# A graph layer's loads, products and exponentials put in another order: staged x ahead of the stores, the first products in hn, a first burst ahead of the second late halves

## What is computed

```python
h = relu(bn(conv1d(xT, conv1_w, pad=0)))               # 1 tap
h = bn(conv1d(h, conv2_w, pad=8))                      # 17 taps
x_conv = relu(h + xT).T
s = x @ w_se.T + b_se                                  # 3 features
dist = sq_i + sq_j - 2 * s @ s.T
A = exp(-dist) * mask
msg = relu(x @ w_msg.T + b_msg)
x_in = concat([x_conv, A @ msg])
gi = x_in @ w_ih.T + b_ih
gh = x @ w_hh.T + b_hh
r, z = sigmoid(gi_r + gh_r), sigmoid(gi_z + gh_z)
n = tanh(gi_n + r * gh_n)
out = layernorm(x + (1 - z) * n + z * x)
```

## Time and profile before

| | |
|---|---|
| median of 3 runs | 332.51 us (330.48 to 332.54) |
| profiled execution | 333.4 us |
| its span, first to last instruction | 331.3 us |
| TensorE busy | 300.3 us (91%) |
| VectorE busy | 248.8 us (75%) |
| ScalarE busy | 154.3 us (47%) |
| mean granted clock of TensorE | 0.977 |
| moved by DMA | 27.21 MB, 82 GB/s over the span |

### The profile page before, as it was taken

How to read it: one execution, slowest core, us unless ns; L and a number is a source line. 1 busy time by engine, 2 the same in 40 slices (tenths; PEclk the granted TensorE clock), 3 DMA queues, 4 the chain that set the end, 5 groups by cost and what they waited for, 6 DMA issues and landing times.

```text
span 331.3 us, 4634 instructions
## 1 busy us (share of the span) xinstructions
PE 300.3 (91%) x1408; PEld 240.1 (72%) x1408; DVE 248.8 (75%) x667; ACT 154.3 (47%) x321; POOL 26.0 (8%) x53
## 2 busy tenths in 40 slices
PE   2859889969999999998999999999999999999970
PEld 1647758748888777886888777887888678888850
DVE  3384869944895996973995996974996996964686
ACT  4564724325776422425876422426776513324440
POOL 3300000000000013000000013000000022000122
PEclk9989999996999999999999999999999999999996
DMA  6600152360121032064120022082110041150002
GB/s 171 249 0 3 28 193 96 85 210 29 59 65 32 32 96 97 33 201 158 57 62 32 32 89 101 32 267 107 61 41 30 32 127 63 38 152 0 0 32 95
DMA packets 12687, 27.21 MB, mean 82 GB/s; under 512 B 1538, under 2 KB 2180, under 8 KB 12548
## 3 DMA queue, kind: packets, MB, share of 16 engines
q1 hardware_dynamic: 12676, 27.08, 24.6%
HBM read 22.88 MB, written 4.19 MB: 82 GB/s over the span
## 4 chain that ended last, share of the span: by engine, by line
PE 56%; DVE 21%; DMA 9%; issue 6%; ACT 4%; SPq 1%; POOL 0%; DVEq 0%; POOLq 0%; ACTq 0%
PE bank L308 54%; DMA xs<-xt_dram 5%; DMA r<-xt_dram 2%; DMA out_dram<-xn 1%; DVE xn L1025 1%; DVE z L960 1%; DVE V_lo L925 1%; DVE H L978 1%; DMA adj<-adj_dram 1%; DVE H L986 1%; PE bank L479 1%; DVE r L960 1%; DVE x_lo L866 1%; DVE EF L990 1%; DVE V_lo L907 1%
## 5 line engine op out<-in xcount | busy, mean ns | idle before, releaser
L308 PE MATMUL bank<-V_hi,cw_hi 128*128 128x512 f32 x160 | 70.8, 442 | 4.5 <-DVE cw_lo L849 3.0
L308 PE MATMUL bank<-V_lo,cw_hi 128*128 128x512 f32 x160 | 64.9, 406 | 0.0
L308 PE MATMUL bank<-V_hi,cw_lo 128*128 128x512 f32 x160 | 64.8, 405 | 0.0
L308 PE MATMUL bank<-x_hi,w_hl 128*128 128x512 f32 x128 | 49.6, 431 | 12.3 <-DVE x_lo L866 12.3
L308 PEld LDWEIGHTS bank<-V_hi,cw_hi 128*128 128x128 f32 x160 | 30.6, 191 | 12.8 <-issue 5.5
L308 PEld LDWEIGHTS bank<-x_hi,w_hl 128*128 128x128 f32 x128 | 25.4, 198 | 19.7 <-DVE x_lo L866 8.0
L308 PEld LDWEIGHTS bank<-V_hi,cw_lo 128*128 128x128 f32 x160 | 30.4, 190 | 8.4
L308 PE MATMUL bank<-c_hi,w_hl 128*128 128x512 f32 x96 | 36.1, 410 | 0.0
L308 PEld LDWEIGHTS bank<-V_lo,cw_hi 128*128 128x128 f32 x160 | 30.6, 191 | 7.3
L308 PE MATMUL bank<-m_hi,w_hl 128*128 128x512 f32 x96 | 35.1, 399 | 0.1
L1129 DVE SCALAR_TENSOR_TENSOR hn<-r,hn 128x512 f32<-128x512 f32 x16 | 11.1, 691 | 23.6 <-ACT hn L653 23.6
(11 more groups left out here) (128 smaller groups left out, 599.3 us busy)
## 6 DMA issues: line engine op xcount, KB each, us to landing
adj<-adj_dram SPq DMA_DIRECT2D x16, 512.0 KB, 5.0
x<-xt_dram SPq DMA_DIRECT2D x16, 256.0 KB, 3.2
xn<-xn_dram SPq DMA_DIRECT2D x16, 256.0 KB, 4.6
out_dram<-xn SPq DMA_DIRECT2D x16, 256.0 KB, 2.2
xs<-xt_dram SPq DMA_DIRECT2D x14, 256.0 KB, 3.6
xn<-wcv_dram SPq DMA_DIRECT2D x1, 1024.0 KB, 6.5
r<-xt_dram SPq DMA_DIRECT2D x2, 256.0 KB, 5.4
adj<-wsm_dram SPq DMA_DIRECT2D x1, 512.0 KB, 8.0
```

What stands on the lines that cost most here:

```text
L308: return nc.tensor.matmul(out, lhs, rhs, start=start, stop=stop, skip_group_check=True)
```

## The change

It has four parts. The first group's P1 is moved from xs to hn. On SP the loads of xs for chunks 0 and 1 of group 1 go ahead of the loop, without the wait for t_ready, and those for group g+2 go behind the last load of x of group g+1, ahead of the late adj loads and of the stores; the loop's body becomes a function, called in a loop of two passes and once behind it. In the GRU stage the loads of xs for chunks 2 and 3 come behind a load of x. On ScalarE the exponentials of batches 0 and 1 go ahead of late_hi(3), and on VectorE mask(0) ahead of residual(3) and mask(1) ahead of late_lo(3); the first group's mix stage keeps its order.

```diff
-        P1_first = xs
+        P1_first = hn
...
             for k in range(NC):
                 load_xn(0, k)
-            with sp.Fori(0, NG - 1) as g:
-                sp.wait_ge(t_ready, 4)
+            for s in range(2):
+                sp.wait_ge(msg_done, 2 * s + 6)
+                load_xs(1, s)
+
+            def group(g, more):
                 for s in range(2):
-                    sp.wait_ge(msg_done, 8 * g + 2 * s + 6)
-                    load_xs(g + 1, s)
                     sp.wait_ge(a_ready, 8 * g + 2 * s + 6)
                     load_adj(g + 1, s)
                 for k in range(NC):
+                    sp.wait_ge(diff_ready, 4 * g + k + 1)
+                    load_x(g + 1, k)
                     if k < 2:
                         sp.wait_ge(msg_done, 8 * g + 2 * k + 10)
                         load_xs(g + 1, k + 2)
-                    sp.wait_ge(diff_ready, 4 * g + k + 1)
-                    load_x(g + 1, k)
+                if more:
+                    for s in range(2):
+                        sp.wait_ge(msg_done, 8 * g + 2 * s + 14)
+                        load_xs(g + 2, s)
                 for pair in range(2, 4):
                     load_adj_late(g + 1, pair)
...
+            with sp.Fori(0, NG - 2) as g:
+                group(g, True)
+            group(NG - 2, False)
...
                 else:
                     late_hi(g, 2)
+                    weights(g, 0)
+                    weights(g, 1)
                     late_hi(g, 3)
                     shared(g, 0, first)
-                    weights(g, 0)
-                    weights(g, 1)
                     operands(g, 1)
...
                     late_lo(g, 2)
+                    mask(g, 0)
                     residual(prev, NC - 1)
+                    mask(g, 1)
                     late_lo(g, 3)
-                    mask(g, 0)
-                mask(g, 1)
+                if first:
+                    mask(g, 1)
```

## The result

The changed kernel takes 323.07 us (median of 4 runs, 321.71 to 323.97), against 332.24 us for the kernel before (4 runs, 330.48 to 332.54). The ratio is 0.9733, 95% interval 0.9687 to 0.9779: 8.9 us faster (7.3 to 10.4). The profiled execution took 323.27 us with a span of 321.0, so 10.3 us of span are gone.

What follows compares the result with a forecast made beforehand. TensorE, busy 300.3 of 331.3 us, was taken to bound the kernel, with time to win in its gaps. Terms 5.7 + 2.0 + 1.65 = 9.4 us off the 332.5 median gave 323.1 us; 8-in-10 range 321.3 to 326.6.

Steps and rivals of the forecast that it cites:

- First pass: Loop's first pass, chunk 0 to next group's convolution: earlier xs load removes gap and clock fall, 5.7 us (5.0 to 6.0).
- Later passes: Same place, passes two and three: xs loads issued earlier end both waits, 1.47 + 0.53 = 2.0 us.
- Bursts: First gather of three bursts: earlier exponentials and masks let it start 0.55 us sooner each, 1.65 us (0 to 2.3).
- The queue's other steps: xs loads for chunks 2 and 3, adj loads, loop copies and first products in hn: cost nothing.
- The sum: All terms, on TensorE: 5.7 + 2.0 + 1.65 = 9.4 us, taken from the median 332.5 to 323.1 us.
- The clock was not down in the median run: Rival, first pass: median run had no clock fall, so 2.6 us less to gain, 325.7 us; chance 0.07.
- Late again: Rival: first group's xs lands as late as before, behind xn and crowded with adj; 5.7 us lost, 328.8 us; chance 0.10.
- The burst gives nothing: Rival, bursts: another wait of the same size stands there, such as operands held by turn_rows; 324.8 us; chance 0.10.
- The other side: Rival: late distances delay late_hi(3) and late_lo(3), conv2's fourth product waits every pass; 10.3 us slower, 342.8 us; chance 0.03.

Runs made afterwards that it cites:

- the second trace: The changed kernel timed again, unaltered, on one chip with three others: 323.25 us, ratio 0.9749 to the kernel before.
- its two halves: The kernel before with the burst's new order on one engine only: ScalarE alone 331.85 us, ratio 0.9987; VectorE alone 330.82 us, ratio 0.9983.
- the two kernels behind adj: The changed kernel with group 1's xs loads interleaved behind adj loads (326.89 us, ratio 0.9846 to before), or behind both (327.97 us, 0.9898).
- the last kernel: The changed kernel with group 1's xs loaded ahead of xn and operands ahead of late_hi(3): 322.68 us, ratio 0.9735 to before; on another chip 321.14 us, 0.9683.

## Why the prediction was right

The forecast of 323.1 us stands beside 323.07. Point by point:

**First pass** (5.7 us, bounds 5.0 and 6.0): the stretch went from 10.21 to 4.35 us, 5.9. The load was issued at 63.83 and not at 65.0: the four xn loads ahead were issued in 1.75 us instead of 2.47, and all of it lay 0.4 us earlier, TensorE as well, so that 0.7 us of the early issue helped. It landed 5.5 us behind its issue, which is the late bound's 5.6 and 0.7 more than the middle (4.8) that the 0.3 was taken from. The one made up for the other, and xs was read at 69.44, inside the bounds of 69.05 to 70.6. That the stall was 0.14 us, and 0.63 in the second trace, against 0.3, is therefore partly luck. That the adj loads behind it slow the landing is not shown; put ahead of xs, they cost about 4 us where their bytes gave 2.6.

**Later passes** (2.0 us): 5.66 to 4.09 is 1.57, and in the third pass 4.72 to 4.09 is 0.63, together 2.2. The sum had taken 4.19 as the stretch without a gap. The wait went to nothing, as argued from gx_done: the copy to x_hi now waits for TensorE and is still in time.

**Bursts** (1.65 us, bounds 0 and 2.3): 3 x 0.66 = 2.0. The mechanism held: the operands, and not the mask, set the start. The step mis-sized was the start of the first exponential: I put it at the end of late_hi(2), and it starts 0.1 us ahead of that end (106.59 against 106.27 + 0.42 = 106.69), so 0.11 is left to wait and not 0.22. Nothing was lost by late_lo(3): no gap stands ahead of conv2's fourth product.

**The queue's other steps** cost nothing, as said: no TensorE wait appears at chunks 1 to 3.

**The sum** came to 9.4; the terms as measured in the profiled executions give 5.86 + 2.20 + 1.98 = 10.0. The span shrank by 10.3, since TensorE also reached the first pass 0.4 us earlier, ahead of anything that was changed. The medians moved by 9.2, or 8.9 by the ratio. That the two ends met so closely is luck in part. Three terms were a little short, together by 0.7 us. Against that the clock's 2.6 us was read from one execution, the 333.4 us one, which was slower than the median. The forecast started from the median but kept the whole 2.6 in the gain, while five other traces with the late load (behind both adj loads, the later passes alone, the burst and its two halves) show 1.3 to 1.6.

An estimate from these figures: if a median execution of the kernel before lost 1.5 us to this fall and not 2.6, each gain read against its trace is 1.1 too large. The changed kernel then gains 10.0 - 1.1 = 8.9 us (measured 8.9), the first pass's loads alone 4.9 - 1.1 = 3.8 (3.8). The kernel with xs behind both adj loads gains 0.3 in the first pass of its trace, 2.2 in the later ones and 2.0 in the bursts, and 4.5 - 1.1 = 3.4 (3.4). It fits all three, but the executions that were not profiled have no trace, so it is not shown.

**The rivals.** "The clock was not down in the median run" was wrong in form: in every trace with the late load the clock fell. By the estimate above, though, 1.1 of its 2.6 us were there. Late again did not come about, and the two kernels behind adj show that it was one place in the queue away: 5.1 and 3.4 us faster than before, where it gave 3.7. "The burst gives nothing" did not come either: alone it is worth 1.7 us (0.8 to 2.6). The other side did not come: late_lo(3) ends at 110.98, well ahead of conv2's fourth product.

**Two slips that changed nothing.** The loads of xs for groups 2 and 3 were forecast near 107 and 180 us and were issued at 102.33 and 174.58; the last load of x that they follow moves up by what the first pass gains. And of the cases priced in the prediction only one, the 342.8, lies above 329.2, not two: late again in full was priced at 328.8.

## What to carry to other kernels

Look at where the busiest engine's few gaps stand and ask of each which queue, not which engine, released it; at the seam of the loop a prefetch that stood behind a wait in its queue cost 3.4 us here, and a fall of the clock besides, and one that stood behind stores and reloads cost 1.5. Give it a buffer that nothing else uses at that time, and issue it before the waits. When a wait has two releasers of almost equal lateness, move both or neither. And a gain read from one profiled execution against a median of others carries what was particular to that execution.

## What the runs showed of the hardware

The price of one fall of TensorE's clock varies with nearly the same gap at the same place. In the kernel before, behind a gap of 3.4 us, the granted clock was at half from 73.5 to beyond 80 us (2.6 us lost). In the kernel with the later passes' loads alone, behind a gap of 2.9 us, it was at half from about 73 to 76.5 (1.4 us lost). In the kernel with the burst alone TensorE stood from 71.5 and went on at 74.60, and the clock fell only at about 75.2 (1.6 us lost). In the second pass of that kernel 2.36 us between two matmuls brought no fall.

The issue of four like loads on the queue also varies from one execution to another: in the last kernel the four loads of xn took 1.76 us in one trace and 2.67 us in the other. And 1 MB more ahead of a load delayed its landing by 3.8 to 4.3 us, where 408 GB/s, the rate of a full window, would have given 2.6.
